# Layer 3's attention: an output matrix in two float32r parts side by side, and the heads' outputs rounded eight heads at a time

## What is computed

```python
ln_out = _ln(hidden_states, ln_w, ln_b)
q  = _ln(_fp8_linear_pertensor(ln_out, wq, wq_scale, q_in_scale).reshape(b, s, g, hpg, d), qln_w, qln_b)
k  = _ln(_fp8_linear_pertensor(ln_out, wk, ...).reshape(b, s, g, d), kln_w, kln_b)
v  = _fp8_linear_pertensor(ln_out, wv, ...).reshape(b, s, g, d)
core = _gqa(q, k, v).reshape(b, s, nh * d)        # 16 query heads of 128, 8 key heads
qx, kx, vx = ...                                   # the same from ln_out and cond, unrounded keys and values
xout = _gqa(qx, kx, vx).reshape(b, s, nh * d)
cat  = jnp.concatenate([core, xout], axis=-1)      # 4096 wide
catq = _div_clamp_fp8(cat, proj_smooth)            # divide, clip at 448, round to bf16, then to fp8 e4m3
return jnp.einsum('bsi,oi->bso', catq, wproj) * (proj_in_scale * proj_w_scale)
```

## Time and profile before

| | us |
|---|---|
| median of 3 runs (2937.60 to 2942.43) | 2940.05 |
| the profiled execution | 2937.88 |
| its span in the trace | 2936.1 |
| own pass, first to last addition to X | 1575.9 to 2002.4 |
| cross pass, first to last addition to X | 2078.0 to 2469.0 |

### The profile page before, as it was taken

The page is one execution under the profiler, slowest core; times in us unless marked ns, Lnnn a source line. Parts: engine busy times, 40 slices in busy tenths (PEclk is TensorE's granted clock), DMA queues, the critical chain, the costliest instruction groups (busy, mean ns, idle before and its releaser), DMA issues. The chain is left out here.

```text
span 2936.1 us, 46383 instructions
## 1 busy us (share of the span) xinstructions
PE 2291.1 (78%) x14566; PEld 1674.8 (57%) x14574; DVE 1847.2 (63%) x3739; ACT 1493.4 (51%) x3353; POOL 1495.4 (51%) x1487
## 2 busy tenths in 40 slices
PE   4788233685897667679739999976999996999997
PEld 2333012344654433268527777764888884788885
DVE  3777378564545535345557888865888875666565
ACT  0667252573120026534348888864888874344443
POOL 5442000631000144158337888863888883788882
PEclk9999665796999769979869999997999997899999
DMA  5232100443021223323220000001000000334343
GB/s 126 66 86 69 52 0 7 141 146 124 34 113 65 52 58 87 76 79 97 67 87 1 0 0 0 0 30 54 6 5 5 4 1 18 89 113 114 101 113 92
DMA packets 119750, 174.63 MB, mean 59 GB/s; under 512 B 25389, under 2 KB 79693, under 8 KB 116383
## 3 DMA queue, kind: packets, MB, share of 16 engines
q1 hardware_dynamic: 119583, 172.53, 20.7%
HBM read 122.49 MB, written 11.48 MB: 46 GB/s over the span
## 5 line engine op out<-in xcount | busy, mean ns | idle before, releaser
L478 DVE TENSOR_REDUCE a_mraw<-a_first_ps 128x4 f32<-128x1024 f32 (+1 forms) x256 | 310.4, 1221 | 148.6 <-PE a_first_ps L329 148.2
L386 ACT ACTIVATE a_et<-a_second_ps 128x1024 f32<-128x1024 f32 x256 | 262.1, 1024 | 160.4 <-PE a_second_ps L347 158.3
L2819 POOL TENSOR_SCALAR a3o_raw<-a3o_raw,a3o_mu,a3o_dev 128x128 f32<-128x128 f32 x320 | 304.6, 964 | 4.8 <-issue 4.8
L2819 POOL TENSOR_SCALAR a3x_raw<-a3x_raw,a3x_mu,a3x_dev 128x128 f32<-128x128 f32 x320 | 283.6, 899 | 4.8 <-issue 4.8
L1669 DVE TENSOR_TENSOR f3e_hidden_low<-f3e_hidden,f3e_hidden_high 128x512 fp32r<-128x512 f32 x96 | 115.9, 1207 | 126.3 <-ACT f3e_hidden_high L1627 125.9
L1538 POOL TENSOR_TENSOR f3e_product<-f3e_silu,f3e_up 128x512 f32<-128x512 f32 x96 | 143.4, 1496 | 73.2 <-PE f3e_u_ps L1554 46.0
L364 PE MATMUL a_o_ps<-a_et,a_vt 128*32 128x256 f32 x2048 | 167.5, 399 | 7.4 <-ACT a_osb L416 6.2
L347 PE MATMUL a_second_ps<-a_qs,a_ks 64*128 64x256 bf16 (+2 forms) x896 | 117.6, 298 | 65.2 <-ACT a_et L386 55.7
L329 PE MATMUL a_first_ps<-a_ks,a_qs 64*128 64x256 bf16 (+2 forms) x1280 | 123.1, 267 | 19.1 <-DMA a_ks<-a_parts 10.3
L347 PEld LDWEIGHTS a_second_ps<-a_qs,a_ks 64*128 64x128 bf16 (+1 forms) x896 | 42.0, 96 | 165.1 <-ACT a_et L386 129.5
L1620 ACT ACTIVATE f3e_silu<-f3e_g_ps 128x512 f32<-128x512 f32 x96 | 57.4, 598 | 144.3 <-PE f3e_g_ps L1554 137.3
(11 more groups left out here) (547 smaller groups left out, 6829.9 us busy)
## 6 DMA issues: line engine op xcount, KB each, us to landing
f_w<-in_f_w SPq DMA_DIRECT2D x16, 1216.0 KB, 8.6
a_qs<-a_parts SPq DMA_DIRECT2D x144, 128.0 KB, 2.4
f_raw<-in_f_w SPq DMA_DIRECT2D x60, 256.0 KB, 3.3
a_ks<-a_parts SPq DMA_DIRECT2D x96, 128.0 KB, 2.4
f3e_spread<-f3e_shares SPq DMA_DIRECT2D x64, 192.0 KB, 3.0
f2e_spread<-f2e_shares SPq DMA_DIRECT2D x36, 256.0 KB, 3.4
f3e_spread<-f3e_shares SPq DMA_DIRECT2D x64, 128.0 KB, 3.0
f_raw<-in_f_w SPq DMA_DIRECT2D x60, 128.0 KB, 3.3
```

The costliest lines, as they stand in the source:

```text
L386: self.nc.scalar.activation(self.et[:, g % self.WAVES_HELD, :, :], self.second_ps[:, :, :], ACT.Exp, scale=self.scale).then_inc(self.e_rea ...
L478: v.tensor_reduce(out, self.first_ps[:, g % 2, :, :].rearrange("p u (c n) -> p u c n", n=N), AX.X, ALU.max).then_inc(self.max_taken, 1)
L2819: mm = nc.gpsimd.tensor_scalar(head, head, mu[:, h:h + 1], dev[:, h:h + 1], ALU.subtract, ALU.mult)
```

## The change

Five things change, all in layer 3's attention.

1. **The output matrix** is cut into two float32r parts, which lie side by side for each of the 16 heads (wparts: 16 x 2 x 256). One matmul of 512 columns gives both parts' products at once, into the two halves of o_ps; a unit has 4 matmuls in place of 12, and `add` adds both halves to X, one after the other. `cut_output` has 2 + 2 operations in place of 4 + 4.
2. **The rounding** handles units 0 and 1 together (round 0), and 2 and 3 together (round 1): 1024 elements per operation instead of 512, written to a float32r catq. `scale` of units 2 and 3 waits until round 0 is done, since each round reads both buffers of cat16; round 1's last operation waits for output 1.
3. **The exponent and magic tiles** are one; both roundings of the own pass share it.
4. **The projection matrices' tiles** are half as wide: 16 tiles of 512 columns per set in place of 8 of 1024 (256 KB a transfer in place of 512 KB). `next_weights` cuts two of them each time.
5. **Both order lists** are written anew.

```diff
-    TILES = 8
+    TILES = 16
+    N = 512
...
-        self.wraw = st.sb("wraw", [P, 2, 1024])
+        self.wraw = st.sb("wraw", [P, 2, self.N])
...
-            catq = sb("catq", [P, 2, 4, P], BF16)
-            wparts = sb("wparts", [P, PARTS, 16, D], BF16)
+            catq = sb("catq", [P, 2, 4, P], F32R)
+            wparts = sb("wparts", [P, 16, 2, D], F32R)
...
                     def output(b, u):
-                        pe.wait_ge(catq_ready, at_batch(b, U, u + 1))
+                        pe.wait_ge(catq_ready, at_batch(b, U // 2, u // 2 + 1))
...
                         for h in range(4):
-                            for p in range(PARTS):
-                                mm = nc.tensor.matmul(o_ps[:, 0:D], catq[:, u % 2, h, :], wparts[:, p, 4 * u + h, :],
-                                                      start=(u == 0 and h == 0 and p == 0),
-                                                      stop=(u == U - 1 and h == 3 and p == PARTS - 1))
+                            mm = nc.tensor.matmul(o_ps[:, :], catq[:, u % 2, h, :],
+                                                  wparts[:, 4 * u + h, :, :].rearrange("p k n -> p (k n)"),
+                                                  start=(u == 0 and h == 0), stop=(u == U - 1 and h == 3))
...
-                        wait(act, catq_ready, at_batch(b, U, max(u - 1, 0)))
+                        wait(act, catq_ready, at_batch(b, U // 2, u // 2))
...
-                    def round_task(b, u):
-                        dve.wait_ge(scaled, at_batch(b, U, u + 1))
+                    def round_task(b, k):
+
+                        dve.wait_ge(scaled, at_batch(b, U, 2 * k + 2))
+                        c16, m = pair(cat16), flat(cmagic)
+                        round_fp8_magic16(nc, c16, m)
                         v.drain()
                         v.tensor_tensor(c16, c16, m, ALU.add)
                         v.drain()
 
-                        wait(dve, multiplied, at_batch(b, U, max(u - 1, 0)))
-                        v.tensor_tensor(flat(catq[:, u % 2, :, :]), c16, m, ALU.subtract).then_inc(catq_ready, 1)
+                        wait(dve, multiplied, at_batch(b, U, 2 * k))
+                        v.tensor_tensor(pair(catq), c16, m, ALU.subtract).then_inc(catq_ready, 1)
 
                     def add(b, k):
                         dve.wait_ge(multiplied, at_batch(b, U, U))
+                        v.scalar_tensor_tensor(cols(self.X, b), o_ps[:, D:2 * D], out_scale[:, 0:1], cols(self.X, b),
+                                               ALU.mult, ALU.add)
+                        v.drain()
...
     CROSS_ORDER = [
...
+        ("a", "exponential", 3), ("a", "normalise", 2), ("c", "turn", 0), ("a", "scale", 1), ("a", "turn", 2),
```

More of the change, by code:

```diff
@@ L2523, with round_fp8_magic16 @@
 HEAD = 128
-def round_fp8_magic16(nc, v16, exponent, magic):
+def round_fp8_magic16(nc, v16, magic):
     v = nc.vector
@@ L2623 @@
-        ("a", "output", 3),
+        ("a", "scores", 0), ("a", "exponential", 0), ("a", "maximum", 0), ("c", "project values", 0),
+        ("c", "keep values", 0), ("r", "rows", 0), ("c", "project values", 1), ("c", "center", 0),
+        ("c", "keep values", 1), ("r", "turn", 0), ("a", "normalise", 0), ("r", "value", 0), ("r", "turn", 1),
+        ("a", "maximum", 1), ("a", "exponential", 1), ("a", "scores", 1), ("a", "turned", 0), ("p", "project", 0),
+        ("c", "center here", 2), ("r", "value", 1), ("a", "turn", 0), ("a", "normalise", 1), ("c", "center", 1),
@@ new lines @@
+        ("p", "project", 1), ("p", "keep", 0), ("a", "maximum", 2), ("a", "scores", 2), ("a", "next weights", 0),
[3 rows of a table added]
+        ("p", "keep", 2), ("a", "scores", 3), ("a", "next weights", 1), ("c", "turn", 1), ("a", "turned", 2),
[3 rows of a table added]
+        ("a", "next weights", 2), ("a", "turn", 3), ("p", "statistics", 2), ("c", "affine", 0), ("a", "apply", 3),
+        ("p", "statistics", 3), ("c", "center", 5), ("a", "output", 1), ("a", "scale", 3), ("p", "statistics", 4),
+        ("c", "turn", 2), ("c", "affine", 1), ("p", "project", 5), ("c", "affine", 2), ("a", "round", 1),
@@ L2624 @@
+        ("c", "turn", 3), ("c", "affine", 3), ("p", "statistics", 5), ("c", "turn", 4), ("a", "next weights", 3),
+        ("p", "keep", 5), ("p", "inverse", 0), ("c", "turn", 5), ("p", "deviation", 0), ("c", "affine", 4),
+        ("a", "output", 2), ("a", "add", 0), ("c", "affine", 5), ("a", "output", 3),
     ]
```

80 lines of the change are left out of this document (34 added, 46 removed), and 38 rows, old and new, of tables (CROSS_ORDER, OWN_ORDER).

## The result

| | before | after |
|---|---|---|
| median of 4 runs each, us | 2938.82 | 2997.79 |
| lowest to highest | 2937.13 to 2942.43 | 2993.16 to 2998.69 |
| the profiled execution, its span | 2937.88, 2936.1 | 2998.41, 2996.5 |
| first to last addition to X, own pass | 1575.9 to 2002.4 | 1580.0 to 2021.4 |
| first to last addition to X, cross pass | 2078.0 to 2469.0 | 2097.2 to 2532.8 |

The ratio is 1.0196, 95% interval 1.0178 to 1.0213: 59 us slower. The time lies inside the forecast's own range (2960 to 3005) and 12 us above its value of 2986. The span grew by 60.4 us: 4.0 by the first own addition, 15.0 in the own pass, 44.6 in the cross pass, 0.2 between them, and 3.4 less behind them.

What follows compares the result with a forecast made beforehand. TensorE was taken to bound the cross pass, VectorE the own pass. Cross 19.5, own 12, half-tile weights 10 and tails 6 sum to 47.5 us on 2937.9; forecast 2986 us, 1.6% slower, range 2960 to 3005 (0.60).

Steps and rivals of the forecast that it cites:

- First gap: Cross batch, after the maximum of unit 1: VectorE waits for unit 1's exponentials on ScalarE, about 1.85 us idle.
- first wait: Cross batch: VectorE's wait for the first exponential, taken to stay as before at 1.57 us.
- Second gap: Cross batch, round 0 to round 1: a 3.55 us scale-apply-scale chain against 2.0 us of VectorE work, 1.6 us idle.
- Maxima: Cross batch: VectorE's idle time for the maxima, put at 0.5 us.
- the walk: Operation durations laid on the new order lists to find waits; in the cross pass 5.5 us idle per batch, before 3.1.
- cross term: Cross pass: batch 27.4 us, 1.3 us more than before, times 15, +19.5 us.
- the tails: Last batch of each pass has nothing to fill with: 2.7 us per pass, +6 us together, bounds +4 and +10.
- The own pass: Layer 3's own pass: +0.8 us per batch, times 15, +12 us; per-batch bounds -0.5 and +1.3.
- The half tiles: Weights at the own pass's start: sixteen half tiles cut instead of eight, +10 us, bounds +7 and +12.
- The first rival: The order fits: the walk's waits are absent in both passes, -31 us there, 2922 us in all; chance 0.19.
- The second: Only the frame grows: passes keep their times, weights and tails stay, 2954 us; chance 0.17.
- The third: Double-size float32r reads and writes slow GpSimd's 20 centerings, the batch passes 28 us: above 3005 us; chance 0.04.

Runs made afterwards that it cites:

- e1: The kernel before with only the projection matrices' tiles halved (16 of 512 columns in place of 8): 2951.78 us, ratio 1.0038.
- e2: The changed kernel with the order lists of the kernel before, rounds at the places of the roundings of units 1 and 3: 3095.07 us, ratio 1.0524.
- e6: The changed kernel with two cross-list entries moved as filler: centering back before unit 1's normalisation, unit 2's statistics behind round 0. 2993.06 us, ratio 1.0181.
- e5: The changed kernel with three cat16 buffers in the cross pass, unit 2's scaling and unit 3's apply moved earlier: 2982.37 us, ratio 1.0143.
- e8: The kernel before with rounding by pairs in bf16 and four cat16 buffers in both passes, old order lists: 3059.13 us, ratio 1.0402.
- e11: The changed kernel with three cat16 buffers, unit 3's turning, copy and apply moved earlier, and centering back at unit 1's wait: 2977.84 us, ratio 1.0124.

## Why the forecast was right, step by step

- **The output product** takes 1.12 us start to start (2203.72 to 2204.84) against 1.31; priced at 1.00. The rows show no wait for outputs 0 and 1 on the path. Outputs 2 and 3, which the prediction had waiting for VectorE, do so in every batch; but in every second one, at the lower clock, VectorE then waits 1.26 us for output 3. That return path was not in the prediction.
- **The rounding.** Priced at 3.6 us a pair; a pair takes 3.62 (mean over 16). The last operation takes 1.23 us (priced 1.2), at 512 elements 0.70. The Trainium skill (VectorE: DVE Perf Modes, "The perf-mode tier table") has tensor_tensor at the single rate in fp32. The formula that the prediction took from the same page stands there in the section "The TRN2 errata"; its estimates are 1.22 and 0.69 us. The trace agrees at both sizes: an fp32r output from bf16 inputs ran at the rate of fp32 here.
- **VectorE's work in the cross pass** fell by 0.27 us, not by 0.5. The rounding gave 1.2 (priced 1.0: the four single ones had cost 8.5 us, not 8.2). Against that the second addition costs 0.57 start to start, the normalisations' products together 0.26 more, statistics and context split 0.16 more.
- **The gaps.** First gap and first wait together: 3.42 forecast, 3.14 measured. Second gap: 1.6 forecast; 1.69 measured, as 1.08 for a3x_cat and 0.61 for `keep` standing behind the waiting scaling. Maxima: 0.5 and 0.75. That is 5.6 of 5.5: the walk was right. Wrong was what I took off it: 0.5 us for hand-overs that would come earlier, of which nothing came. With 22.7 of work that is 28.3 us, the time of a batch in the kernel with three zero matmuls.
- **What the walk did not have** is TensorE's clock: 0.57 us per batch, VectorE's wait for the output. I had written that TensorE would have gaps, and priced them at nothing. The cross term of +19.5 us was mis-sized by these three and by 0.1 of the gaps: 0.5 + 0.3 + 0.6 + 0.1 = 1.5 us per batch; with the last batch (4.3 us longer than its counterpart, of which I had put 2.7 into the tails) it is +44.6.
- **The own pass**: +0.8 us per batch forecast, 0.8 measured over the eight batches (0.7 over whole pairs). Its parts were other ones: work +0.04 (forecast -0.5), idle +0.8 (forecast +1.3). The table load, too, was to add about 1 us to every second batch before and after; after, it is covered. A batch without it is 1.1 us longer than before, one with it 0.3. So the match of the pass is in part luck. The last two batches are 4.9 us longer, by the half tiles and the tail: +15.0 in all for +12 and half of the tails' 6.
- **The half tiles**: +10 us forecast up to the pass's start; with nothing else changed 9.6 in e1's trace, and 10 between the medians, which hold the cutting of the second set as well. In the changed kernel the new own list gives 6 us of it back before the first addition (e2 against after). The landing was 2.8 us (median), right at the limit that the prediction had named as its sign of being wrong, and not 3.3: I had taken the row of another tensor. The estimate by the Trainium skill (DMA: Bandwidth & Descriptors, "Anatomy of one DMA"), 2.6 us, was the nearer one here; for the full tile the row's 4.2 us stood against its 3.2. The page gives that fit for transfers issued by GpSimd, and these are issued by SyncE, so neither figure tests it.
- **The first rival** (the order fits) fell: the waits of the walk are there. Filler (e6) and buffers (e5, e8) do not close the gaps, and from round 0 to round 1 it is 3.77 us with 2.05 as with 2.7 us of filler. The 3.5 us at which the rival was to decide were not tried. Where the second gap all but closed (e11), more than half of the time came out at other waits. **The second** (only the frame grows) would have needed steady batches of before. **The third** (GpSimd) is there in small and off the path: from 2183 to 2415 us its centerings take 0.955 us each in place of 0.902, 1 us per batch, but it waits 46.9 us for the variances, before 30.0.
- **The sum.** The span grew by 60.4 us where the terms add up to 47.5. The cross pass took 22 us more than its term and its tail, the start 6 less, and the stretch behind the layer 3.4 less, for which I have no reason. So that the time lies 12 us above the forecast owes something to errors that cancel.
- **What I had not asked**: which of the five edits costs. Added in this order, by the medians: half tiles 10 us; output matrix another 33; pairs with the new lists another 14. The forecast had the output matrix as the saving on TensorE and the pair as a saving on VectorE; the first is a loss by VectorE's work, the second by its waits.

## To carry to other kernels

An edit that relieves the full engine is worth what the next engine has left, work and round trips together. Here the next one was idle for 3 us of 26, all of it waits on round trips, and 1.5 us more to do made the batch 1.0 us longer. Joining two steps of a pipeline into one saves their overhead and makes the first half wait for the second and everything behind it wait for both: price the chain through the other engines from the end of one joint step to the start of the next (here 3.8 us), and compare it with the filler that stands there. Filler taken from elsewhere is not free: it had hidden a wait where it stood.

## What was not expected of the hardware

TensorE stood still for 1.01 and 0.64 us, with four 128-column transpositions between, and was granted the lower of its two clocks (0.50, 1.2 GHz) for the next 3 us or so; with 0.92 and 0.43 us in the next batch it was not, and in e6 it was not with 1.01 and 0.56 us either. The 8 matmuls behind took 3.5 us in place of 2.1. Three matmuls that add zero, two behind the first gap and one in the second, kept the clock at 1.00 (2.4 GHz) and made the kernel 9 us faster. A loop in which TensorE has just lost a little work can so run alternately at two speeds, and a change that seems to help may only have kept the clock: read the granted clock of both kernels before giving a gain to the edit. The Trainium skill (TensorE: Matmul & The Clock Gate, "HAM oscillation — how this bites in real kernels") describes such an oscillation for waits for DMA; here the waits were for VectorE and ScalarE, and it came in every second batch.
